# The attention's adjacency counts, held in two PSUM banks by halves of their columns

## The reference, cut to what matters

```python
# L0, for each of 8 relations, over the edges of that type and a self-loop per node
e = leaky_relu(s[src] + d[dst]); m = segment_max(e, dst); w = exp(e - m[dst])
out += segment_sum(w / denom[dst] * h[src], dst)
# L1 (L2 gathers over the same edges)
out_deg = clip(segment_sum(ones, src), 1)
feat_n = feat * rsqrt(out_deg)
copy_sum = segment_sum(feat_n[src], dst)
# L2
agg = segment_sum((x @ W_msg[i])[src], dst)
```

## Time and profile before

| What | us |
|---|---|
| median of three runs | 4038.57 |
| profiled execution, its own time | 4019.43 |
| its span | 4017.7 |
| attention's loop, as the window of 200 to 1825 us | 1625 |

### The profile page before, as it was taken

How to read it: one execution, slowest core, us unless ns; L and a number is a source line. 1 busy time by engine, 2 the same in 40 slices (tenths; PEclk the granted TensorE clock), 3 DMA queues, 4 the chain that set the end, 5 groups by cost and what they waited for, 6 DMA issues and landing times. The chain is left out here.

```text
span 4017.7 us, 77702 instructions
## 1 busy us (share of the span) xinstructions
PE 2872.7 (72%) x16134; PEld 2016.3 (50%) x16135; DVE 2334.3 (58%) x8562; ACT 1464.6 (36%) x3326; POOL 2316.7 (58%) x1835
## 2 busy tenths in 40 slices
PE   7167777767777676655879949788777877788752
PEld 4045555555555555442434436666666656566531
DVE  6288888888888888765342244444444444444423
ACT  1055455445554555432000014334333333333320
POOL 0276666666666666540000008888888888888880
PEclk8555555565555555556989969898888988988876
DMA  3433433433343334882532315555555555555543
GB/s 126 98 105 100 119 106 102 113 106 106 98 118 106 97 106 116 75 123 94 173 100 75 99 19 57 54 53 54 53 54 54 52 53 54 54 52 54 54 41 78
DMA packets 651839, 336.53 MB, mean 84 GB/s; under 512 B 436752, under 2 KB 612163, under 8 KB 650820
## 3 DMA queue, kind: packets, MB, share of 16 engines
q0 software_dynamic: 148736, 86.57, 22.4%
q1 hardware_dynamic: 443062, 112.07, 13.5%
q10 hardware_dynamic: 59856, 136.11, 8.9%
HBM read 156.42 MB, written 202.84 MB: 89 GB/s over the span
## 5 line engine op out<-in xcount | busy, mean ns | idle before, releaser
L2110 POOL DMA_INDIRECT sums<-el_rows,el_idx x816 | 1270.2, 1557 | 648.1 <-DVE el_rows L2324 399.7
L811 POOL DMA_INDIRECT at_hs<-table,at_rec_s x976 | 1038.8, 1064 | 605.0 <-issue 284.9
L952 PE MATMUL near_ps<-at_pair_hot,at_src_low_hot 128*128 128x425 f16 x976 | 503.4, 516 | 468.8 <-ACT at_count_s L849 293.9
L849 ACT CAST at_count_s<-near_ps 128x400 f16<-128x400 f32 x976 | 482.5, 494 | 887.9 <-PE near_ps L952 379.1
L2322 DVE CAST el_idx<-el_place 128x4 uint32<-128x4 f32 x204 | 35.4, 173 | 844.0 <-DMA sums<-el_rows,el_idx 802.0
L924 PEld LDWEIGHTS sums_ps<-at_hw,at_hit 128*128 128x128 f32 x1952 | 471.5, 333 | 34.4 <-issue 28.9
L924 PE MATMUL sums_ps<-at_hw,at_hit 128*128 128x66 f32 x1952 | 442.5, 408 | 8.3 <-DVE acc L998 8.3
L952 PEld LDWEIGHTS near_ps<-at_pair_hot,at_src_low_hot 128*128 128x128 f16 x976 | 128.1, 131 | 608.2 <-ACT at_count_s L849 355.2
L990 DVE TENSOR_SCALAR at_pair_hot<-iota_wide,at_rec_s 128x400 f16<-128x400 f16 x976 | 322.8, 333 | 1.5
L2258 ACT ACTIVATE el_h<-el_h_ps,el_valid 128x128 f32<-128x128 f32 x816 | 233.2, 368 | 240.8 <-PE el_h_ps L2172 169.6
L2126 PE MATMUL el_miss_t<-ident_b,el_miss 128*128 128x128 bf16 x816 | 84.9, 266 | 311.8 <-DVE el_miss L2296 311.8
(11 more groups left out here) (355 smaller groups left out, 5134.3 us busy)
## 6 DMA issues: line engine op xcount, KB each, us to landing
slots<-at_count_s ACTq DMA_DIRECT2D x122, 850.0 KB
el_rec<-attr SPq DMA_DIRECT2D x816, 32.0 KB
chunk<-slots SPq DMA_DIRECT2D x240, 100.0 KB
attr<-in_edge_attr SPq DMA_DIRECT2D x19, 1248.0 KB
chunk<-slots ACTq DMA_DIRECT2D x224, 100.0 KB
at_rec_s<-meta SPq DMA_DIRECT2D x992, 3.5 KB
at_hs<-table,at_rec_s POOLq DMA_INDIRECT x976
el_pair<-meta SPq DMA_DIRECT2D x816, 1.0 KB
```

The lines of the kernel that those rows point to most:

```text
L811: pool.indirect_dma_start(hs[:, s, u, :], None, k.table, bass.IndirectOffsetOnAxis(rec[:, s, u, 0:1].bitcast(U32), 0)).then_inc(gathered[s ...
L849: a.copy(count[:, (n.o + d) % 2, i, 0:AW], near[:, (n.o + d) % 2, 0:AW]).then_inc(count_ready, 1)
L952: pe.matmul(near[:, s, 0:SW], low_hot[:, s, i, :], pair_hot[:, s, i, :], start=False, stop=True, skip_group_check=(i > 0)).then_inc(near_r ...
L2110: pool.indirect_dma_start(k.sums_flat[a], bass.IndirectOffsetOnAxis(idx[:, j, a:a + 1], 0), rows[:, j, a, :], None, compute_op=ALU.add).th ...
```

## The change

The tile `near` keeps its two banks, but they no longer stand for two batches: bank 0 takes columns 0 to 207 (`LW = 208`), bank 1 columns 208 to 424, the 25 degree columns among them. Each visit's matmul becomes two, each copy becomes two, and each half has its own pair of semaphores (`left_ready`/`left_copied`, `near_ready`/`count_ready`). The carries become four matmuls. The degrees are copied by ScalarE into an SBUF tile `deg` once per batch, behind its last copy, and VectorE adds them from there; the carries of the right half wait for that copy.

```diff
+LW = AW // 32 * 16 + 16
+        deg = sb("deg", [P, 2, NT])
             def keep(n, d, i):
+                s = (n.o + d) % 2
...
+                act.wait_ge(left_ready, n(B, d * B + i + 1))
+                a.copy(count[:, s, i, 0:LW], near[:, 0, 0:LW]).then_inc(left_copied, 1)
                 act.wait_ge(near_ready, n(B, d * B + i + 1))
-                a.copy(count[:, (n.o + d) % 2, i, 0:AW], near[:, (n.o + d) % 2, 0:AW]).then_inc(count_ready, 1)
+                a.copy(count[:, s, i, LW:AW], near[:, 1, 0:AW - LW]).then_inc(count_ready, 1)
+            def degrees(n, d):
+                if n.after(2 - d):
+                    act.wait_ge(deg_added, n(1, d - 1))
+                a.copy(deg[:, (n.o + d) % 2], near[:, 1, AW - LW:SW - LW]).then_inc(deg_copied, 1)
             def store(n, d):
+                act.wait_ge(left_copied, n(B, d * B + B))
                 act.wait_ge(count_ready, n(B, d * B + B))
...
                     keep(n, 1, 7)
+                    degrees(n, 1)
                     store(n, 1)
...
-                if n.after(1 - d):
-                    pe.wait_ge(count_ready, n(B, d * B))
-                    if n.after(2 - d):
-                        pe.wait_ge(deg_added, n(1, d - 1))
-                else:
-                    pe.wait_ge(run_start, 5)
-                for i in range(2):
-                    pe.matmul(near[:, s, 0:SW], k.carry_by[:, i, :],
-                              count[:, past, bass.ds(at[i], 1), :].rearrange("p i c -> p (i c)"), start=(i == 0), stop=False)
+                rows = count[:, past]
+                for h, (c0, c1) in enumerate(((0, LW), (LW, SW))):
+                    if n.after(1 - d):
+                        pe.wait_ge(count_ready if h else left_copied, n(B, d * B))
+                        if h:
+                            pe.wait_ge(deg_copied, n(1, d))
+                    else:
+                        pe.wait_ge(run_start, 5)
+                    for i in range(2):
+                        pe.matmul(near[:, h, 0:c1 - c0], k.carry_by[:, i, :],
+                                  rows[:, bass.ds(at[i], 1), c0:c1].rearrange("p i c -> p (i c)"), start=(i == 0), stop=False)
             def counts(n, d, i):
                 if i:
+                    pe.wait_ge(left_copied, n(B, d * B + i))
+                pe.matmul(near[:, 0, 0:LW], low_hot[:, s, i, :], pair_hot[:, s, i, 0:LW], start=False,
+                          stop=True, skip_group_check=(i > 0)).then_inc(left_ready, 1)
+                if i:
                     pe.wait_ge(count_ready, n(B, d * B + i))
-                pe.matmul(near[:, s, 0:SW], low_hot[:, s, i, :], pair_hot[:, s, i, :], start=False,
+                pe.matmul(near[:, 1, 0:SW - LW], low_hot[:, s, i, :], pair_hot[:, s, i, LW:SW], start=False,
                           stop=True, skip_group_check=(i > 0)).then_inc(near_ready, 1)
...
-                    dve.wait_ge(count_ready, n(B, B))
-                    v.tensor_tensor(k.out_deg[:], k.out_deg[:], near[:, s, AW:SW], ALU.add).then_inc(deg_added, 1)
+                    dve.wait_ge(deg_copied, n(1, 1))
+                    v.tensor_tensor(k.out_deg[:], k.out_deg[:], deg[:, s], ALU.add).then_inc(deg_added, 1)
```

More of the change, by code:

```diff
@@ L741, in attention @@
                                                   [sem("count_written0"), sem("count_written1")])
-        deg_added, dst_copied = sem("deg_added"), sem("dst_copied")
+        left_ready, left_copied = sem("left_ready"), sem("left_copied")
+        deg_copied, deg_added, dst_copied = sem("deg_copied"), sem("deg_added"), sem("dst_copied")
         iota_ready, run_start, passed = sem("iota_ready"), sem("run_start"), sem("passed")
@@ L844, in keep @@
             def keep(n, d, i):
+                s = (n.o + d) % 2
                 if i == 0 and n.after(2 - d):
-                    act.wait_ge(count_written[(n.o + d) % 2], n.pairs(d) * 16)
+                    act.wait_ge(count_written[s], n.pairs(d) * 16)
+                act.wait_ge(left_ready, n(B, d * B + i + 1))
+                a.copy(count[:, s, i, 0:LW], near[:, 0, 0:LW]).then_inc(left_copied, 1)
                 act.wait_ge(near_ready, n(B, d * B + i + 1))
-                a.copy(count[:, (n.o + d) % 2, i, 0:AW], near[:, (n.o + d) % 2, 0:AW]).then_inc(count_ready, 1)
+                a.copy(count[:, s, i, LW:AW], near[:, 1, 0:AW - LW]).then_inc(count_ready, 1)
[3 more added lines that the diff above has]
+                a.copy(deg[:, (n.o + d) % 2], near[:, 1, AW - LW:SW - LW]).then_inc(deg_copied, 1)
             def store(n, d):
+                act.wait_ge(left_copied, n(B, d * B + B))
                 act.wait_ge(count_ready, n(B, d * B + B))
```

## The result

| | before | changed kernel |
|---|---|---|
| median of 4 runs each, same chip | 4039.16 us (4037.94 to 4045.41) | 4078.48 us (4072.28 to 4083.13) |
| ratio | 1 | 1.0093, 95% interval 1.0076 to 1.0110 |
| profiled execution, span | 4019.43, 4017.7 | 4082.95, 4081.1 |
| granted clock over the span | 0.733 | 0.75 |

The change costs 39 us where I forecast a gain of 22. (The profiled pair lies 64 us apart, since the profiled execution of before was 20 us quicker than its median and the other 4 us slower than its own. So shares are read from the traces, and sizes from the medians.) Of those 64 us the attention, from the first `at_top` reduction to the last, took 1668.2 for 1609.7 us. Another 7 went into the later stage that loads the stored counts back, whose code the change does not touch.

What follows compares the result with a forecast made beforehand. Two equal rings, VectorE's 11.66 us per batch and the count-copy chain's 11.63, plus late completions, were taken to bound it; terms of -0.39 in 51 of 112 steps over 122 batches gave 22 us, so 4017, range 3935 to 4105.

Steps and rivals of the forecast that it cites:

- the side to which I gave 0.26: The outcome that the changed kernel is slower, made of rivals B, C and a little of A.
- Term 1: Count 4 to its copy: the left half is done 217 columns sooner, so 0.60 becomes 0.42 us, -0.18 per batch.
- the work of TensorE: Where sums or transposes stand between counts, TensorE's work is as long as before, so 6.34 us per batch stay.
- Term 2: Copy 4 to copy 7: 3.28 for 3.36 us, -0.08, with ScalarE the limit and a pair of copies costing 0.46.
- rival B: Slower by ScalarE at copies 4 to 7: pairs that do not overlap, 65 us more, 4103 us; chance 0.15.
- Term 3: Copy 7 to the next count 0, with degrees' copy and right carries: 1.20 for 1.33 us, -0.13.
- The whole chain: Counts and copies of a batch, TensorE and ScalarE: terms sum to -0.39 us, 11.63 becomes 11.24.
- VectorE takes the gain: VectorE's 11.66 us per batch stays, so steps where it does not wait gain nothing; in rival A, chance 0.18, nothing measurable.
- Rival C: Slower by late handovers: two TensorE completions per visit, second set late half as often, 4121 us; chance 0.09.
- Rival D: Much faster: chain catches up behind late completions or clock rises; 211 us at most (3828), half of it 3933; chance 0.20.

Runs made afterwards that it cites:

- joined_copy: Changed kernel with split matmuls of 200 and 225 columns, but one copy reading both banks on one completion: 4075.61 us, 1.0095 of the kernel before, holding chip.
- one_event_again: Changed kernel, both copies of a visit started on the right half's event, no event for the left; repeated on a holding chip: 4057.73 us, 1.0099 of before.
- one_event: Changed kernel, both copies of a visit started on the right half's event, no event for the left; quiet chip: 3911.01 us, 0.9957 of before.
- long_loop: Changed kernel with the attention's loop written out for twelve batches a turn instead of six: 4064.85 us, 1.0124 of the kernel before, holding chip.
- two_copies: Kernel before with whole matmuls of 425 columns, but ScalarE copies 208 and then 192 elements: 4062.01 us, 1.0061 of the kernel before, holding chip.

## Why the prediction was wrong

The time of 4078.48 lies in the range of 3935 to 4105, on the side to which I gave 0.26. Point by point:

- **Term 1 and the work of TensorE** were right: count to copy 0.42 in the median (forecast 0.42), counts 1.99 and 1.21 apart where sums and transposes stand between them (1.96 and 1.21).
- **Term 2** had the price of a pair right: 0.44 between starts (forecast 0.46, rival B from 0.56 on). The bound of 0.37 was too low, that of 0.69 too high. The 0.08 it was to save did not come. Counts 4 to 7 took 0.81 + 1.06 + 1.14 = 3.01 in the medians of the quiet chip, where before needed 1.15 + 1.01 + 1.08 = 3.24, but there copies 5 and 6 stood 0.67 and 0.73 behind their counts, since ScalarE was busy. Copy 4 to copy 7 is 3.18 for 3.17, and the second half of `hit_t`, for which VectorE waits, starts 2.60 behind copy 4 for 2.45: term 1's 0.18 is all but used up there.
- **Term 3** was half right: copy 7 to the next count 0 fell from 1.33 to 1.27 in the medians of the pair at the top (forecast 1.20). The right carries start 0.25 behind the end of the degrees' copy, not 0.15.
- **The whole chain**: the 25th percentile of the batches at the top fell from 11.63 to 11.40 us, 0.23 of the forecast 0.39, about what terms 1 and 3 come to as measured (0.18 + 0.06).
- **VectorE takes the gain** when nothing is late: right, and on quiet chips it is all that happens (0.9983).
- **The failing step** is the sentence "The late completions I leave as they are." I had put 1.7 us per batch down to them, more than four times the gain I was counting, and then took them for a constant. By copies later than 0.6 us behind their counts, with what the quiet chip shows for the same kernel taken off, they are 239 - 81 = 158 us before and 340 - 97 = 243 us after. That is 85 us in 106 batches, 0.8 us in each, against 0.2 to 0.4 gained; the batch grew by 0.47. (This sizes the loss and no more: joined_copy pays the whole price with a sum that is hardly larger.) Part of it moved to where it costs most: of the copies of visit 6, in front of the half of `hit_t` that VectorE waits for, .50 are late instead of .31.
- **Rival C** had the place and the sign (4121 us, for 4078), but not the mechanism: one_event_again has half the completions and is as slow, and joined_copy has the whole price with one completion per visit. I had argued against C that "what holds up the one would mostly hold up both at once". The rows bear that out: the left copies wait 273.8 us for "remote", the right ones 14.0, and of 157 late left copies for which both semaphores' records are there, 108 have the two within 0.1 us of each other. It did not matter, since the first alone became late more often.
- **Rival D** named the right size of the prize: without held completions before takes 3928, 111 us less than 4039, close to D's half (105). That was luck, since the half was a guess, and no split of the counts gets it.
- **A sign that misled.** I had said that C would show in idle time of the copies for "remote" and "issue" clearly over 430 us. It is 273.8 + 133.9 + 14.0 + 6.2 = 427.9. The label tells who came last by the profile and not how late; the start of a copy against its count does. A mean clock other than 0.56 was to be another sign, and it came out at 0.59; but on the quiet chip it is 0.60 before and 0.59 after (300 to 1700 us), so it says nothing of the change. (In the earlier trace rows the first slice stands at 8 tenths and the 18 behind it at 5 or 6; the prediction read the 18 as the first.)

What is shown: the late copies come with GpSimd's gathers, go away without them, move along with them, start as soon as their semaphore moves, and are more, or at costlier visits, when the counts are split in two matmuls. What is not: what delays the semaphore, why one chip does it and another doesn't, and why two matmuls of half the columns meet it more often than one. The traces of the holding chips also lack a part of the records (693 of the left counts' 976 semaphore records in the changed kernel at the top, 975 on the quiet chip), so the taking of the profile may have a part in it; no run here separates the two. No version here is shown to be best on both kinds of chip: one_event has the lowest ratio on a quiet one (0.9957, but not side by side with the changed kernel's 0.9983) and loses 1% on a holding one.

## What to carry to other kernels

If the trace shows an engine that starts late after everything visible is done, find what those starts have in common before costing a change around them: here it was worth four times the terms that I summed, and the change moved it. Shortening a chain of handovers between TensorE and ScalarE pays only up to the engine that runs beside it (0.2% here), and a split costs its second instruction everywhere. Compare kernels side by side, and on more than one chip, when the difference is under a few per cent, since the same edit came out at 0.9957 on one chip and 1.0099 on another.

## What the runs showed of the hardware

- Semaphores that TensorE's counts raise moved 1 to 4 us late while GpSimd ran indirect gathers, on two chips of five and in the comparison at the top. In the changed kernel there the late copies started a median 1.1 us (middle half 0.7 to 1.25) after the end of the last gather; those in time have 1.1 too (middle half 0.4 to 2.0), so this distance alone shows little. Where completions were held, the kernel before took 88 to 111 us more than its 3928; not all of that need be the gathers, since with one gather instead of eight 15 us were left between two such chips (3863.99 and 3848.50).
- Two copies from PSUM of 208 and 192 elements are 339 and 335 ns long in the rows and start 0.23 apart; the next instruction starts 0.21 behind the second. One of 400 elements is 494 ns long and holds ScalarE for about 0.37.
- An indirect gather of 128 rows kept GpSimd busy for 1.06 to 1.07 us in the mean where a batch has eight, and for 1.49 where it has one; a plain load of as many rows took 0.54. This is the loads' group of the kernel with plain loads, 300 to 1700 us:

```profile
L811 POOL DMA_DIRECT2D at_hs<-table x878 | 472.1, 538 | 861.5 <-PE near_ps L950 773.2 <-issue 86.9
```

- TensorE's mean granted clock was 0.56 before and 0.59 after in 300 to 1800 us of the pair at the top, and the kernel was slower all the same. On the quiet chip it was 0.60 and 0.59, so twice the matmuls for as many columns did not raise it there.
- The stage that reads the stored counts back took 377.4 to 380.5 us in the kernels with split counts or split copies (373.8 in long_loop) and 367.4 to 370.5 in all others, on both kinds of chip, though its code was the same. It is not the split of the matmuls, since two_copies has whole ones and took 378.2. In the changed kernel and in two_copies TensorE's matmuls there fall behind in two steps of 3 to 4 us, at the same two places of the stage. Its cause was not looked for.
